# Base projection and adapter projection share three PSUM banks; output tile in a buffer of its own; attention values split first; next tile normalised inside the routing and transposed mid-tile

## What is computed

```
x1 = x + ga * (attn @ wo)                                   # per row of 1024
h  = layernorm(x1) * (1 + cb) + sb
base = h @ W_base.T + b_base                                # 1024 outputs
gate = softmax(h @ W_gate.T)                                # 8 experts
thr  = sigmoid(h @ W_thr + b_thr) * 0.125
w    = max(gate - thr, 0);  w = w / sum(w)   (1 where the sum is 0)
moe  = (einsum(h, A_w) * w) @ B_w * 2                       # 8 experts of rank 16: 128 columns
out  = x1 + gb * (base + moe)
```

## Time and profile before

| | before |
|---|---|
| median of three runs | 1616.33 us |
| the profiled execution | 1615.49 us |
| its span in the trace | 1613.7 us |
| TensorE busy | 1554.2 us, 96% of the span |
| ScalarE / VectorE / GpSimd busy | 64% / 58% / 38% |
| mean granted TensorE clock | 0.988 of full |
| phase B, first matmul of tile 0 to the end | 1180.0 to 1613.7 us |

### The profile page before, as it was taken

One profiled execution on the slowest core, in us unless ns is written; L12 is line 12 of the kernel. 1 busy time (PEld: TensorE's weight loads), 2 busy tenths in 40 slices (PEclk: granted clock), 3 DMA queues, 4 the chain that ended last, 5 costly groups with the idle time before them and its releaser, 6 DMA issues.

```text
span 1613.7 us, 29453 instructions
## 1 busy us (share of the span) xinstructions
PE 1554.2 (96%) x9530; PEld 1184.5 (73%) x9530; DVE 938.8 (58%) x2868; ACT 1039.8 (64%) x2718; POOL 605.5 (38%) x477
## 2 busy tenths in 40 slices
PE   5899999999999999999999999998989999999996
PEld 3667777777777777777777777775678888888885
DVE  4737666665766655666666566665655444454533
ACT  2548899999999889999999899898421111010100
POOL 3425254353533414334334234245123434343332
PEclk9999999999999999999999999998999999999998
DMA  9883443545434483343243333345322121212110
GB/s 346 286 247 80 104 112 99 146 126 133 129 86 105 118 249 75 79 102 84 61 107 81 77 86 83 82 153 154 77 93 79 39 78 40 79 40 78 39 65 27
DMA packets 172035, 174.44 MB, mean 108 GB/s; under 512 B 21044, under 2 KB 120676, under 8 KB 171896
## 3 DMA queue, kind: packets, MB, share of 16 engines
q1 hardware_dynamic: 169784, 168.54, 37.3%
q10 hardware_dynamic: 2112, 4.19, 0.7%
HBM read 96.65 MB, written 25.18 MB: 75 GB/s over the span
## 4 chain that ended last, share of the span: by engine, by line
PE 71%; ACT 6%; issue 6%; DVE 6%; DMA 5%; POOL 5%; SPq 1%; ACTq 0%; DVEq 0%; POOLq 0%
PE ps_qkv L1273 14%; PE ps_s L1273 13%; PE ps_s L1317 8%; PE ps_pv L1344 8%; PE ps_t L1286 7%; PE ps_s L721 7%; PE ps_s L692 3%; PE ps_qkv L692 3%; ACT probsT L1593 2%; ACT rows_sb L1557 1%; DMA x<-in_L_attn_x_dram 1%; POOL h_lo L924 1%; DMA x_start<-in_L_attn_x_dram 1%; DMA out_dram<-x 1%; DMA stk<-rot 1%
## 5 line engine op out<-in xcount | busy, mean ns | idle before, releaser
L1557 ACT ACTIVATE rows_sb<-rows_sb,bias_m 128x640 f32<-128x640 f32 (+7 forms) x512 | 396.1, 774 | 12.5
L1827 DVE CUSTOM_DVE_ANT_0 rows_sb<-ps_t,mask 128x512 f32<-128x512 f32 (+3 forms) x512 | 297.5, 586 | 160.5 <-PE ps_t L1286 152.9
L1286 PE MATMUL ps_t<-stk 96*128 96x512 f32 (+3 forms) x768 | 267.5, 350 | 5.2 <-DMA stk<-rot 1.8
L1593 ACT ACTIVATE probsT<-ps_s 128x512 f32<-128x512 f32 (+1 forms) x488 | 243.5, 537 | 32.7 <-PE ps_s L1317 16.7
L1317 PE MATMUL ps_s<-stk 98*128 98x512 f32 (+3 forms) x768 | 222.9, 371 | 1.3 <-DMA stk<-m_rows 1.1
L1853 DVE TENSOR_TENSOR ps_s<-ps_s,mask_t 128x128 f32<-128x128 f32 (+1 forms) x384 | 120.9, 341 | 166.4 <-PE ps_s L1317 162.9
L1286 PEld LDWEIGHTS ps_t<-stk 96*128 96x128 f32 x768 | 145.4, 190 | 51.6 <-DVE m_rows L1843 10.2
L1989 POOL TENSOR_TENSOR rope_b<-rope_b,rope_sin 128x512 f32<-128x512 f32 x64 | 82.8, 1294 | 266.5 <-DVE rope_b L1812 266.5
L1317 PEld LDWEIGHTS ps_s<-stk 98*128 98x128 f32 x768 | 132.1, 191 | 67.7 <-issue 30.8
L766 ACT ACTIVATE gsm<-ag_out,bthr 128x1 f32<-128x1 f32 x16 | 4.7, 294 | 248.1 <-DVE ag_out L853 248.1
L1827 DVE CUSTOM_DVE_ANT_0 rows_sb<-ps_t,mask,smax_part 128x128 f32<-128x128 f32 (+3 forms) x256 | 140.8, 550 | 38.9 <-PE ps_t L1286 11.3
(11 more groups left out here) (218 smaller groups left out, 3160.2 us busy)
## 6 DMA issues: line engine op xcount, KB each, us to landing
stk<-rot SPq DMA_DIRECT2D x384, 128.0 KB, 2.4
probsT<-in_L_wmod_dram SPq DMA_DIRECT2D x5, 2048.0 KB, 9.3
wm_one<-in_L_wmod_dram SPq DMA_DIRECT2D x5, 2048.0 KB, 10.9
w_raw<-in_L_attn_wq_dram SPq DMA_DIRECT2D x16, 512.0 KB, 4.0
w_raw<-in_L_attn_wk_dram SPq DMA_DIRECT2D x16, 512.0 KB, 4.7
w_raw<-in_L_attn_wv_dram SPq DMA_DIRECT2D x16, 512.0 KB, 4.1
attn_scratch<-attn_sb SPq DMA_DIRECT2D x128, 64.0 KB, 2.9
h_scratch<-h_pair SPq DMA_DIRECT2D x32, 256.0 KB, 3.2
```

Source lines behind the costliest of these rows:

```text
L1286: pe.matmul(bank[:, 0:c1 - c0], stk[0:3 * HD, u % 2, 0, qt // 4, h, qt % 4 * P:(qt % 4 + 1) * P], stk[0:3 * HD, u % 2, 1, part, h, 0:c1 - ...
L1557: act.activation(row, row, ACT.Exp, bias=bias_m[:, qt, h:h + 1], scale=SCALE, accum_out=sums[:, qt // 4, h, qt % 4:qt % 4 + 1]).then_inc(s ...
L1593: act.activation(probs[PROBS[w]][:, hs[0]:hs[-1] + 1, 0:n], s_bank[(NS * u + k) % 3][:, 0:len(hs) * n].rearrange("p (h n) -> p h n", h=len ...
L1827: dve.tensor_tensor_reduce(rows_sb[:, to, at + c0:at + c1], bank[:, 0:n], mask[:, BANK - n:BANK] if last else mask[:, 0:1].broadcast_to([P ...
```

## The change

In short:

- PSUM: instead of 512 + 138, then 512 columns, the product with h is made in three groups c = 0, 1, 2 in three banks: 394 columns (256 of W_base and the 138 of ag, from one buffer "wa"), 384 and 384 (buffer "wb"). In group 0 the base and the adapter part come from one matmul. The product with B_w has nine matmuls (three of 256, six of 384 columns); on bank 0 it starts anew, since VectorE has taken base plus bias out of that bank before, into y_base.
- The finished tile is written to the buffer spare and stored from there; GpSimd waits for the store before. SyncE issues the load of x for tile i + 2 first, without waiting for the store, then the store, then (top of the next body) the load of the attention values.
- ScalarE and GpSimd split the attention values at the top of their bodies, ahead of the exponentials and ahead of the rsqrt.
- VectorE normalises the next tile inside the routing, right after the maximum and y_base, ahead of the wait for the exponentials. TensorE transposes it between group 1 and group 2.
- One operation on single elements of the routing has another form. Buffers of phase B lie elsewhere; in the preparation VectorE waits once for the last stores of attention output before it writes a piece of the weights.

```diff
@@ SyncE, body
                 sp.wait_ge(out_ok, i + 2)
+                if has_next2:
+                    load_x1(sp, i + 2, e)
                 if not has_next:
                     sp.wait_ge(last_ok, 1)
-                sp.dma_start(out_rows[bass.ds(i * P, P), :], x1[:, e, :]).then_inc(out_st, 16)
-                if has_next2:
-                    sp.wait_ge(out_st, 16 * i + 16)
-                    load_x1(sp, i + 2, e)
+                sp.dma_start(out_rows[bass.ds(i * P, P), :], spare[:, :]).then_inc(out_st, 16)
@@ rest_weights
                 dve.wait_ge(st_hi, n + 1)
+                if (kind, k, half) == ("wb", KT // 2, 1):
+                    for x in range(2 * PAIRS - 2, 2 * PAIRS):
+                        chunk_stored(dve, x)
@@ TensorE, body  (WA = 256, WB = 384, AGW = 138, BANK = 512)
-                for c in range(0, D, BANK):
+                for c in range(3):
+                    if c == 2 and has_next:
+                        turn_xn(pe, i + 1)
+                    n = WB if c else WA + AGW
+                    cols = slice((c - 1) * WB, c * WB) if c else slice(0, n)
+                    his, los = (wb_hi, wb_lo) if c else (wa_hi, wa_lo)
                     for kt in range(KT):
...
+                        w_hi_, w_lo_ = (w[kt // 4][:, kt % 4, cols] for w in (his, los))
+                        for way, (h, w) in enumerate(((h2_hi, w_hi_), (h2_hi, w_lo_), (h2_lo, w_hi_))):
+                            mm = pe.matmul(ps_all[:, c * BANK:c * BANK + n], h[:, kt, :], w,
+                                           start=(kt == 0 and way == 0),
+                                           stop=(c == 0 and kt == KT - 1 and way == 2))
...
                 pe.transpose(ps_pv[:, 0:P], hw[:, :, :].rearrange("p e r -> p (e r)"), ident[:, :]).then_inc(hwT_ok, 1)
-                if has_next:
-                    turn_xn(pe, i + 1)
                 pe.wait_ge(hwT_hi_ok, i + 1)
                 pe.wait_ge(hwT_lo_ok, i + 2)
...
+                for c in range(3):
+                    cols = slice(WA + (c - 1) * WB, WA + c * WB) if c else slice(0, WA)
+                    mm = three(pe, ps_all[:, c * BANK:c * BANK + (WB if c else WA)], hwT_hi[:, :], hwT_lo[:, :],
+                               bt_hi[:, cols], bt_lo[:, cols], c == 0, True)
@@ ScalarE, body
+                if has_next2:
+                    split_a(act, i + 2)
                 act.wait_ge(ag_cp, i + 2)
...
-                if has_next2:
-                    split_a(act, i + 2)
                 act.wait_ge(hwT_ok, i + 1)
@@ route
                 dve.tensor_reduce(nm, ag_out[:, ER:ER + E_], AX_X, ALU.max, negate=True).then_inc(gate_max, 1)
+                dve.tensor_tensor(y_base[:, :], ps_all[:, 0:WA], bias[:, 0:WA], ALU.add)
+                between()
                 dve.wait_ge(gate_exp, 2 * i + 1)
...
-                then(dve.scalar_tensor_tensor(wd, ws, 0.0, ws, ALU.is_equal, ALU.add))
+                then(dve.tensor_scalar(wd, ws, 0.0, ws, ALU.is_equal, ALU.add))
@@ VectorE, body
-                route(i)
-                if has_next:
-                    norm(dve, i + 1, 1 - e)
+                route(i, lambda: norm(dve, i + 1, 1 - e) if has_next else None)
...
+                dve.tensor_tensor(xn[:, 0:WA], ps_all[:, 0:WA], y_base[:, :], ALU.add)
                 if has_next:
-                    dve.tensor_tensor(xn[:, :], ps_s[0][:, :], bias[:, :], ALU.add).then_inc(y_ev, 1)
+                    dve.tensor_tensor(xn[:, WA:D].rearrange("p (c n) -> p c n", c=2),
+                                      ps_all[:, BANK:3 * BANK].rearrange("p (c n) -> p c n", c=2)[:, :, 0:WB],
+                                      bias[:, WA:D].rearrange("p (c n) -> p c n", c=2), ALU.add).then_inc(y_ev, 1)
@@ GpSimd, body
+                if has_next2:
+                    split_a(i + 2)
                 if has_next:
                     rsqrt(i + 1)
-                if has_next2:
-                    split_a(i + 2)
...
                 pool.wait_ge(y_gated, i + 1)
-                pool.tensor_tensor(x1[:, e, cols], x1[:, e, cols], xn[:, cols], ALU.add).then_inc(out_ok, 1)
+                pool.wait_ge(out_st, 16 * i + 16)
+                pool.tensor_tensor(spare[:, cols], x1[:, e, cols], xn[:, cols], ALU.add).then_inc(out_ok, 1)
```

More of the change, by code:

```diff
@@ L31 @@
 AGW = ER + 10
+WA, WB = 2 * P, 3 * P
 MODC = 6 * D // BANK
@@ L249, in psum @@
             return outer.enter_context(nc.psum_tensor(name, [P, cols], F32))
-        ps_s = [psum("ps_s0", 2 * BANK), psum("ps_s1", 2 * BANK)]
+        ps_all = psum("ps_s", 4 * BANK)
+        ps_s = [ps_all[:, 0:2 * BANK], ps_all[:, 2 * BANK:4 * BANK]]
         ps_t = [psum("ps_t0", BANK), psum("ps_t1", BANK)]
@@ L312, in adaln_block @@
         h_pair = sb("h_pair", [P, 2, BANK], F32)
+        sb("pad", [P, 40], F32)
         h_next, h_next_hi = h_pair[:, 0, :], h_pair[:, 1, :]
@@ L360, in adaln_block @@
         wo_hi = sb2("wo_hi", [P, KT, D], F32R)
-        wb_hi = sb2("wb_hi", [P, KT, D], F32R)
+        wb_hi = [sb2("wb_hi0", [P, KT // 2, 2 * WB], F32R)]
+        h2_hi = sb2("h2_hi", [P, KT, P], F32R)
+        wb_hi.append(sb2("wb_hi1", [P, KT // 2, 2 * WB], F32R))
+        h2_lo = sb2("h2_lo", [P, KT, P], F32R)
         wo_lo = sb2("wo_lo", [P, KT, D], F32R)
-        wb_lo = sb2("wb_lo", [P, KT, D], F32R)
+        wb_lo = [sb2("wb_lo0", [P, KT // 2, 2 * WB], F32R)]
+        wa_hi = [sb2("wa_hi0", [P, KT // 2, WA + AGW], F32R)]
+        wa_lo = [sb2(f"wa_lo{half}", [P, KT // 2, WA + AGW], F32R) for half in range(2)]
+        hw = sb2("hw", [P, E_, R_], F32)
+        hwT_hi = sb2("hwT_hi", [P, P], F32R)
+        hwT_lo = sb2("hwT_lo", [P, P], F32R)
+        sb2("gap", [P, 8], F32)
         gb = sb2("gb", [P, B, D], F32)
@@ L370, in adaln_block @@
         a_lo = sb2("a_lo", [P, KT, P], F32R)
-        ag_hi = sb2("ag_hi", [P, KT, AGW], F32R)
-        ag_lo = sb2("ag_lo", [P, KT, AGW], F32R)
         bt_hi = sb2("bt_hi", [P, D], F32R)
         bt_lo = sb2("bt_lo", [P, D], F32R)
[L375 to L381, removed]
+        wa_hi.append(sb2("wa_hi1", [P, KT // 2, WA + AGW], F32R))
+        wb_lo.append(sb2("wb_lo1", [P, KT // 2, 2 * WB], F32R))
         x1 = sb2("x1", [P, 2, D], F32)
@@ L386, in adaln_block @@
         h2t = sb2("h2t", [P, BANK], F32)
-        hwT_hi = sb2("hwT_hi", [P, P], F32R)
-        hwT_lo = sb2("hwT_lo", [P, P], F32R)
+        gsm = sb2("gsm", [P, 48], F32)
+        bthr = sb2("bthr", [P, 2], F32)
+        ag_out = sb2("ag_out", [P, AGW], F32)
+        y_base = sb2("y_base", [P, WA], F32)
         stage = [x[:, a * BANK:(a + 1) * BANK] for x in (gb[:, 0, :], gb[:, 1, :], bias[:, :], spare[:, :]) for a in range(2)]
@@ L531, in piece @@
         def piece(kind, k, half):
-            ks = slice(4 * half, 4 * half + 4)
+            if kind == "wb" and k * P < WA:
+                return tuple(w[half][:, :, k * P:(k + 1) * P] for w in (wa_hi, wa_lo))
             if kind == "wb":
-                return tuple(w[:, ks, k * P:(k + 1) * P] for w in (wb_hi, wb_lo))
+                return tuple(w[half][:, :, k * P - WA:(k + 1) * P - WA] for w in (wb_hi, wb_lo))
             if kind == "bt":
@@ L538, in piece @@
                              for w in (bt_hi, bt_lo))
-            return tuple(w[:, ks, slice(0, ER) if k == 0 else slice(ER, AGW)] for w in (ag_hi, ag_lo))
+            return tuple(w[half][:, :, slice(WA, WA + ER) if k == 0 else slice(WA + ER, WA + AGW)] for w in (wa_hi, wa_lo))
         def piece_cols(kind, k):
@@ L729, in body @@
                 pe.transpose(ps_pv[:, 0:P], hw[:, :, :].rearrange("p e r -> p (e r)"), ident[:, :]).then_inc(hwT_ok, 1)
-                if has_next:
-                    turn_xn(pe, i + 1)
                 pe.wait_ge(hwT_hi_ok, i + 1)
                 pe.wait_ge(hwT_lo_ok, i + 2)
-                for c in range(0, D, BANK):
-                    mm = three(pe, ps_s[0][:, c:c + BANK], hwT_hi[:, :], hwT_lo[:, :], bt_hi[:, c:c + BANK],
-                               bt_lo[:, c:c + BANK], False, True)
+                for c in range(3):
+                    cols = slice(WA + (c - 1) * WB, WA + c * WB) if c else slice(0, WA)
+                    mm = three(pe, ps_all[:, c * BANK:c * BANK + (WB if c else WA)], hwT_hi[:, :], hwT_lo[:, :],
+                               bt_hi[:, cols], bt_lo[:, cols], c == 0, True)
                 mm.then_inc(y_ok, 1)
@@ L837, in modulate, with route @@
                     modulate_half(j, b, half)
-            def route(i):
+            def route(i, between):
                 done = [0]
@@ L852, in route @@
                 dve.wait_ge(ag_ok, i + 1)
[L853 removed]
+                dve.tensor_copy(ag_out[:, :], ps_all[:, WA:WA + AGW]).then_inc(ag_cp, 1)
                 dve.wait_ge(ag_cp, i + 2)
                 dve.tensor_reduce(nm, ag_out[:, ER:ER + E_], AX_X, ALU.max, negate=True).then_inc(gate_max, 1)
+                dve.tensor_tensor(y_base[:, :], ps_all[:, 0:WA], bias[:, 0:WA], ALU.add)
+                between()
```

(19 more changed lines are left out.)

2 lines of the change are left out of this document (1 added, 1 removed).

## The result

The changed kernel takes 1678.62 us (median of six runs, 1670.84 to 1685.03), the kernel before beside it 1616.64 us: ratio 1.0367, 95% interval 1.0344 to 1.0391 (the two medians alone give 1.0383, inside it). The profiled execution took 1681.86 us, its span is 1680.1 us.

What follows compares the result with a forecast made beforehand. TensorE, busy 96% of the span, was taken as the bound, with a second path nearly as long. 1613.7 + 40 (wait) + 4.5 (tile 0) - 0.8 (ends) + 22 (clock) gave 1679.4 us span, 1681 us time; range 1640 to 1708.

Steps and rivals of the forecast that it cites:

- The last step of the sum: From the forecast span of 1679.4 us to the time: profiled execution 1.8 us above span, 0.8 below median, giving 1681.
- TensorE's work: Phase B, per tile: three matmul groups take 13.0 us instead of 13.87; with moved transposes TensorE's sum is 27.3 us.
- The merge is paid back by the move: TensorE, per tile: narrower matmul groups save 0.9 us, the next tile's transposes cost 0.9 us in their new place.
- The values' landing: Steady tiles: attention values land 19.8 us after T, the start of the transpose of hw; bounds 18.7 and 20.3.
- the 1.3 us for the store ahead: SyncE's queue: the store, put between x and the attention values, delays the values' landing by 1.3 us.
- The 5.7 us for x and the values by themselves: Transfers without the store between: attention values land 5.7 us after the issue of x.
- The norm and T to T: Steady tiles: norm done at T+25.2, next transpose of hw (T) at T+30.4; 3.1 us more in 13 tiles, 40 us.
- The clock: TensorE's 3.0 us gap lowers its clock in 8 of 13 tiles, 2.8 us each: 22 us, bounds 0 and 36.
- Tile 0: First tile of phase B: longer chain plus VectorE's add of x held by GpSimd's split, 4.5 us, between 2.3 and 7.5.
- The 2.3 us for the longer chain: Tile 0: statistics, rsqrt, norm, transposes and group 2 after the add of x cost at least 2.3 us more.
- The ends: Last two tiles: no values are split, no idle before the end, tile 15 saves 0.9 us; together -0.8 us.
- Rival 4: Steady tiles: values land early and narrow matmuls lose their overhead, saving 18 us, to 1598 us; chance 0.04.

Runs made afterwards that it cites:

- e1: The changed kernel with GpSimd's rsqrt for the next tile put back before its split of the attention values; 1621.52 us, ratio 1.0014.
- e3: The changed kernel with GpSimd's rsqrt first again and the next tile's transposes back behind that of hw; 1604.21 us, ratio 0.9907.
- e7: The changed kernel with SyncE's queue order x, attention values, store instead of x, store, values; loop peeled; 1665.17 us, ratio 1.0287.
- e4: The changed kernel with twelve unused matmuls of 512 columns filling TensorE's wait before the mid-tile transposes; 1664.29 us, ratio 1.0273.
- e2: The changed kernel with the next tile's transposes back behind that of hw, values still split first; 1614.36 us, ratio 0.9971.
- e5: The changed kernel with the load of the attention values issued a body earlier, ahead of the wait for the finished tile; 1620.37 us, ratio 0.9998.
- e10: The changed kernel with rsqrt first, transposes late, values loaded a body earlier and ScalarE's split back behind the exponentials; 1603.98 us, ratio 0.9900.

## Why the prediction was right, and where it was not

The predicted 1681 us, the direction and the mechanism hold. Part of the closeness is luck: the span was forecast at 1679.4 us and came at 1680.1, but 4.1 us of that lie ahead of phase B, where nothing was forecast, and phase B came out 3.4 us shorter than forecast. The last step of the sum also slips: 1679.4 + 1.8 + 0.8 is 1682, not 1681. Step by step:

- **TensorE's work.** The groups take 4.35 + 4.2 + 4.2 = 12.75 us instead of the 13.0 I took; the lower value I had worked out by columns (12.8) was the right one. A matmul of 384 columns follows at 0.174 us. TensorE's sum with the transposes in mid-tile is 27.07 us (e1), 27.3 in the prediction. "The merge is paid back by the move" is shown by e1 and e3: 0.9 us lie between 27.07 and 26.17, and e1 stands at 1.0014.
- **The values' landing.** T+19.8 forecast, ScalarE starts at T+19.9. Of its parts, the 1.3 us for the store ahead hold: the store lands 1.3 us behind x, and without it there the values come 1.1 us closer behind x (e7). The 5.7 us for x and the values by themselves were a little short: they took 6.2 on average in e7, x 4.1 of them where it took 3.5 before. (The 0.83 us for the rsqrt are 0.81 by the rows.)
- **The norm and T to T.** Transposes at T+25.2 (24.76 to 25.51), as forecast; T to T without a clock fall 30.3 us (e4), forecast 30.4. Over 13 tiles 37.9 us, forecast 40. That this wait comes from the order in GpSimd's queue is shown by e1, that it needs the transposes in mid-tile by e2, that it needs the late values by e5.
- **The clock.** 21.1 us by e4, forecast 22, as a product of two wrong factors, and so by luck: it fell in 10 tiles, not 8, and cost 2.1 us each, not 2.8. A long low stretch, like that of the earlier trace rows, did cost 2.7 us; but half of the stretches lasted only 3.4 us (window above) and cost 1.5.
- **Tile 0.** +4.4 us, forecast 4.5, and the step failed. I had VectorE's add of x held by GpSimd's split. The trace shows the add at its usual 1.22 us, and GpSimd's split at 2.70 us instead of 2.40:

```profile
1193.44 1.22 DVE L819 TENSOR_TENSOR x<-x,xn 128x1024 f32<-128x1024 f32 x1
...
1194.17 2.70 POOL L942 TENSOR_TENSOR a_lo<-a_raw,a_hi 128x1024 fp32r<-128x1024 f32 x1 [16.25 <-ACT a_hi L767]
```

  The rsqrt, behind the split, so begins at 1196.83, 0.5 us after the statistics. Another 1.6 us are the clock: the wait before the transposes is 4.16 us there, and from the transposes to T it takes 6.7 us, 5.1 at the full level (e1). The 2.3 us for the longer chain are what is left. VectorE is held where it comes second, as in tile 0 of e1, whose norm takes 2.82 us instead of 0.81 and ends behind GpSimd's split, so that T of tile 0 comes 2.3 us later there than after:

```profile
1197.22 2.34 POOL L942 TENSOR_TENSOR a_lo<-a_raw,a_hi 128x1024 fp32r<-128x1024 f32 x1
...
1197.29 2.82 DVE L830 TENSOR_SCALAR xn<-x,mv,rstd 128x1024 f32<-128x1024 f32 x1 [0.24 <-POOL rstd L938]
```

  So the one that came second waited. The Trainium skill's rule on the shared SBUF interfaces (GPSIMD Engine Reference, Specifications) fits the two that overlapped in tile 0: the add has two SBUF inputs.
- **The ends.** -1.1 us, forecast -0.8.
- **Rival 4** and the figure of the Trainium skill beside it (TensorE: Matmul & The Clock Gate, Back-to-back issue gap: N/2.4 + 2.5 ns, given there for a single matmul by itself; 162.5 at 384 columns is an estimate by it): the runs give 174 ns, 12 ns more. Even e3 and e10, with no wait left, reach 1604 us and not 1598.

## What to carry to other kernels

When an instruction is moved to the front of an in-order queue, ask when its input arrives, and what short instruction will stand behind it: here 0.8 us of rsqrt, ready at the moment when the values landed, waited 3.5 us for the two splits of values that it did not need. Moving work is free only where it fills a wait; the eight transposes had filled one, and the place they left stayed open. And count the clock when TensorE gets a wait of some 2 us or more: filling it with useless matmuls was worth 1% here.

## What the runs showed of the hardware that was not expected

- The lower clock does not need a long pause. Waits of 1.98 to 2.11 us were followed by a fall in some tiles and by none in others (e7), those of 2.6 us and more by one in 10 of 13 tiles after. The length of the wait alone does not decide: the three without a fall had waits of 2.95, 2.98 and 3.32 us, longer than some with one. No mid-tile wait of up to 1.87 us was followed by a fall in these two runs. The low stretches came in two lengths, about 3.4 and 6.9 us.
- A VectorE operation on 8 elements can take as long as GpSimd's instruction beside it: 2.14 us in the earlier trace rows, 1.67 us at another line in e1 (L880, row above), 0.23 to 0.29 us in the changed kernel, where GpSimd has nothing to do at that time. Operations on single elements beside the same split keep their 0.15 to 0.17 us.
- Three transfers of 512 KB, issued in one queue within 1.3 us, landed in the order of issue, at spacings that belong to the transfer: 1.3 us for the store (after and e7), 1.9 to 2.1 us for the values. Taking the store out of their way gained the values 0.9 us. The first of the three, x, landed 3.5 us after its issue where the next issue stood 0.7 us behind it (before), and 3.9 to 4.1 us where it stood 0.5 us behind (after, e5, e7).
